# A chunked-softmax attention on one core: keys dealt over the key tiles so that one weight tile serves a whole head

## The chip, the cores and the metric

The kernel runs on one core of a Trainium2 chip. Its time is the device time in microseconds, from the first to the last instruction of that core with what the launch adds, as the median of several runs. Engines: TensorE (PE, with its weight loads as PEld), VectorE (DVE), ScalarE (ACT), GpSimd (POOL), and SyncE (SP), whose queue issues the DMAs that matter here.

## The reference, cut to what matters

Two layers of a small transformer over 2 batches of 1024 tokens, width 128, all in float32. The change is in the attention of the first layer: 16 heads of width 64, of which each group of four shares one key and value head, and the softmax is not over all 1024 keys but inside each chunk of 64 keys.

```
q = (x @ w_q.T) ; k = (x @ w_k.T) ; v = (x @ w_v.T)        # 16 heads of q, 4 of k and v
kc, vc = k, v cut into C = 16 chunks of 64 keys
scores = einsum('bhqd,bhckd->bhcqk', q, kc) * 64 ** -0.5
w = softmax(scores, axis=-1)                               # inside each chunk
chunk_out = einsum('bhcqk,bhckd->bhcqd', w, vc)
sum_w = w.sum(axis=-1, keepdims=True)
out = (chunk_out * sum_w).sum(axis=2) / (sum_w.sum(axis=2) + 1e-09)
```

So each key of a chunk gets the same factor for a given query: a number per (chunk, query), made of the sum of that chunk's exponents and of the total over the chunks. Behind this attention come a soft mixture of experts, a causal attention and a routed mixture, which the change leaves alone.

## The kernel before, in words

One loop runs over the two batches. In it the first attention runs over 16 heads (`head0` on TensorE and VectorE, `head` on ScalarE), each over 8 key tiles of 128 keys. Keys lie on the partitions of the score tiles, the 1024 queries on the free axis. Nothing schedules the work but the order in which each engine's program is written, and semaphores.

What one head costs, and where it is written (lines of the kernel before):

- Maxima: for each of 16 units (a tile of 128 queries by 512 keys) one fp32r matmul (L750, two PSUM banks in turn) and one VectorE reduction to 8 chunk maxima (L1919). Head i works on the units of head i+1, two units after each key tile. Eight transposes (L757) turn them into 16 rows, which ScalarE copies under the queries (L1460).
- Scores of key tile t: two matmuls of the high parts (L771) and two of the low parts with the chunk maxima (L776), then one exponent over 128x1024 on ScalarE (L1502) into EE.
- Chunk sums: at the head's end 16 float32 matmuls of 512 columns with 32 columns of weights (L786), four at a time in the four column groups of the array, since each key tile holds two other chunks. A float32 matmul is two instructions in the profile.
- Normalisers: ScalarE copies the sums out (L1482, 512 columns), four transposes (L796), seven small VectorE operations (L1928 to L1940), four transposes back (L803), a ScalarE copy into `r_rows` (L1477, 512 columns).
- Weights: SP writes `r_rows` into the DRAM tensor `weight_rows` (L503, four DMAs), waits for them (L523/L524), and reads them back spread over partitions: for each key tile two rows, each broadcast to 64 partitions, 256 KB a DMA, 16 DMAs and 4 MB a head (L515), into a ring of four tiles. From the fifth tile on a load waits until VectorE has used the tile it replaces (L512).
- Weighing: VectorE multiplies each EE tile by its weight tile (L1948), tiles 0 to 3 of head i-1 in head i at t = 5 and 7, tiles 4 to 7 in head i+1 at t = 1 and 3. TensorE then sums the values (L814, float32), ScalarE copies them out (L1468).
- Projections of what is needed next stand in the heads at t = 3 and t = 5: queries (L677) in heads 0, 2, 4, ..., keys (L682, two float32 matmuls of 512 columns, moving operand `att_in`) in heads 1, 5, 9, values (L688, eight float32 matmuls, `att_in` as the stationary operand, 64 columns moved) in heads 3, 7, 11. The first group's stand ahead of head 0. The high and low parts of the keys are split on ScalarE (L1448) and VectorE (L1903).

Behind head 15 come its normalisers, the last 12 weighings and values, and the output projection (L881).

Of the kernel before, what the change touches and what calls it, by code (L numbers as in the profile page):

```python
# [12 lines left out]
AX = mybir.AxisListType.X  # L13
ds = bass.ds


P = 128
NB = 2
T = 1024
# [16 lines left out]
CQ = NC // 2  # L36
# [3 lines left out]
              "eps_row": NT, "chunk": 4 * 32}  # L40
# [26 lines left out]
def layer_program(nc, A, out, sorted_in, sorted_out, weight_rows):  # L67
    ctx = ExitStack()
    with ctx:
# [16 lines left out]
        chunk_sum = const("chunk").rearrange("p (a c) -> p a c", a=4)  # L86
# [53 lines left out]
        weight_ring = [v[:, :, :].rearrange("p t d -> p (t d)").rearrange("p (o q) -> p o q", o=2) for v in V1]  # L140
# [15 lines left out]
        S_sb = own0[:, 2 * BANK:3 * BANK]  # L156
        r0 = sb("r0", [P, 4, 4, CQ])
        sw = sb("sw", [P, 4, 4, CQ])
        r1 = sb("r1", [P, 4, 4, CQ])
        tot = sb("tot", [P, 4, 2])  # L160
        rp = sb("rp", [P, 4, 4, 32])
        r_rows = sb("r_rows", [P, BANK])
# [201 lines left out]
        wt_in = [sem(f"wt_in{i}") for i in range(4)]  # L364
# [84 lines left out]
        def _(sp):  # L449
# [33 lines left out]
            with sp.Fori(0, NB) as b:  # L483
                for L in range(2):
                    if L == 0:
# [11 lines left out]
                        def weight_rows_out(i):  # L497

                            sp.wait_ge(s_rr, b * HEADS + i + 1)
                            sp.sem_inc(s_held, 1)  # L500
                            for j in range(4):
                                half, odd = divmod(j, 2)
                                sp.dma_start(weight_rows[i % 2, odd * CQ:(odd + 1) * CQ, half * BANK:(half + 1) * BANK],  # L503
                                             r_rows[32 * j:32 * j + CQ, :]).then_inc(wr_in, 16)
# [16 lines left out]
                        for i in range(HEADS):  # L521
# [3 lines left out]
                            for a in range(4):  # L525
                                if a == 3 and i % GH == GH - 1 and i // GH + 2 < GROUPS:
                                    next_group(i // GH + 2)
                                weight_tiles_in(i, a)
# [102 lines left out]
        def _(pe):  # L631
# [31 lines left out]
            def attention0(b):  # L663
# [3 lines left out]
                krows = HD + NC  # L667
                h0 = b * HEADS
# [68 lines left out]
                def maxima(i, units):  # L737
# [3 lines left out]
                    for x in units:  # L741
# [8 lines left out]
                        pe.matmul(banks(5 + x % 2, BANK), Q_HIGH[u][:, t * P:(t + 1) * P], KA[g % 2][:, half * BANK:(half + 1) * BANK],  # L750
# [29 lines left out]
                def chunk_sums(i, a):  # L780
# [1804 lines left out]
```

## Time and profile before

| | |
|---|---|
| median of 3 runs | 2207.07 us (2201.11 to 2214.0) |
| the profiled execution's own time | 2210.59 us |
| its span, first to last instruction | 2208.5 us |
| granted TensorE clock, mean | 0.932 |
| first attention, batch 0 | about 22 to 532 us, batch 1 about 1110 to 1618 us |

The page's first part says how busy each engine is, part 4 what the chain of work that ended last ran through, and part 5 the costliest groups of instructions with the idle time in front of them. Idle time counts only where the engine is the one that others wait for.

### The profile page before, as it was taken

How to read it: one execution, taken by the hardware profiler on the slowest of the kernel's cores; microseconds unless marked ns; L12 is line 12 of the kernel's file. 1: busy time of each engine (PE TensorE's matmuls, PEld its weight loads, DVE VectorE, ACT ScalarE, POOL GpSimd, SP SyncE). 2: the span in 40 equal slices, each digit the busy share in tenths (PEclk: the TensorE clock that was granted, in tenths of full speed). 3: DMA queues.
4: the chain of work that ended last, by engine and by line, in shares of the span. 5: the costliest groups of instructions: out<-in, count | busy, mean ns of one | idle time of the engine just before them, and what ended most of it. 6: DMA issues, size and time to landing. Idle time of an engine off the chain costs nothing.

```text
span 2208.5 us, 32078 instructions
## 1 busy us (share of the span) xinstructions
PE 1976.8 (90%) x10106; PEld 1193.3 (54%) x10106; DVE 1440.1 (65%) x2492; ACT 980.7 (44%) x1377; POOL 586.5 (27%) x549
## 2 busy tenths in 40 slices
PE   6899999996997999998888999999979889999985
PEld 4444444444784655556644444444448755655554
DVE  7677788865327777753467887778561377777443
ACT  3444454441224666662334444444413246656422
POOL 0000000000101798884120000000010047897921
PEclk7999999998887999998879999999979879999987
DMA  2366665567000000000516565656750000000024
GB/s 94 84 154 160 155 149 141 139 161 237 24 1 10 2 10 6 1 1 30 163 39 154 141 146 141 146 141 151 182 198 1 1 10 10 1 6 1 1 79 135
DMA packets 84846, 187.99 MB, mean 85 GB/s; under 512 B 17697, under 2 KB 46754, under 8 KB 83106
## 3 DMA queue, kind: packets, MB, share of 16 engines
q1 hardware_dynamic: 83650, 183.76, 32.8%
q0 software_dynamic: 1024, 2.10, 0.3%
q8 instruction: 88, 1.44, 0.3%
q14 instruction: 84, 0.69, 0.1%
HBM read 178.47 MB, written 8.91 MB: 85 GB/s over the span
## 4 chain that ended last, share of the span: by engine, by line
PE 67%; DVE 14%; issue 9%; ACT 3%; DMA 3%; POOL 2%; SPq 1%; DVEq 0%; another core or an unknown queue 0%; POOLq 0%; ACTq 0%
PE PS L814 10%; PE PS L786 5%; PE PS L750 5%; PE PS L986 4%; PE PS L926 4%; PE PS L966 3%; DVE mx L1919 3%; PE PS L881 3%; PE PS L969 3%; PE PS L1159 3%; PE PS L771 3%; PE PS L776 3%; PE PS L1218 2%; DMA V<-weight_rows 2%; POOL Esum L2463 2%
## 5 line engine op out<-in xcount | busy, mean ns | idle before, releaser
L1919 DVE TENSOR_REDUCE mx<-PS 128x8 f32<-128x512 f32 x512 | 329.6, 686 | 178.7 <-PE PS L750 164.0
L2463 POOL TENSOR_TENSOR Esum<-Esum,EE 128x512 f32<-128x512 f32 (+3 forms) x320 | 341.3, 1094 | 15.5 <-POOL Esum L2463 10.5
L1948 DVE TENSOR_TENSOR EE<-EE,V 128x1024 f32<-128x1024 f32 x256 | 303.1, 1219 | 45.3 <-DMA V<-weight_rows 44.7
L1502 ACT ACTIVATE EE<-PS 128x1024 f32<-128x1024 f32 x256 | 259.9, 1024 | 142.7 <-PE PS L776 141.2
L2052 DVE TENSOR_REDUCE mrow<-PS 128x1 f32<-128x512 f32 (+3 forms) x384 | 204.1, 552 | 99.1 <-PE PS L929 69.9
L2405 POOL TENSOR_TENSOR QA<-hT,QA 128x512 fp32r<-128x512 f32 x2 | 2.6, 1282 | 996.5 <-ACT hT L1690 996.5
L814 PE MATMUL PS<-EE,Vlater 128*64 128x512 f32 x1024 | 250.5, 609 | 9.4 <-ACT U L1468 8.3
L750 PE MATMUL PS<-KA,QA 128*128 128x512 f32 x512 | 204.1, 454 | 31.8 <-DVE mx L1919 25.8
L1586 ACT ACTIVATE EE<-PS 128x1024 f32<-128x1024 f32 (+2 forms) x192 | 138.1, 739 | 121.4 <-PE PS L969 118.7
L771 PE MATMUL PS<-QA,KA 128*128 128x512 f32 x512 | 185.1, 443 | 0.0
L750 PEld LDWEIGHTS PS<-KA,QA 128*128 128x128 f32 x512 | 97.8, 196 | 130.3 <-DVE mx L1919 88.4
L776 PE MATMUL PS<-QB,KB 80*128 80x512 f32 x512 | 163.1, 400 | 0.0
L986 PE MATMUL PS<-EE,V 128*64 128x512 f32 (+3 forms) x640 | 131.2, 522 | 0.0
L2077 DVE COPY_PREDICATED EE<-consts,F 128x256 f32<-128x256 int32 x96 | 95.3, 992 | 47.9 <-ACT EE L1586 47.8
L814 PEld LDWEIGHTS PS<-EE,Vlater 128*64 128x64 f32 x1024 | 61.8, 136 | 115.3 <-issue 92.4
L786 PE MATMUL PS<-EE,consts 128*32 128x512 f32 x1024 | 116.5, 595 | 0.8 <-DVE QA L1896 0.8
L771 PEld LDWEIGHTS PS<-QA,KA 128*128 128x128 f32 x512 | 91.9, 192 | 42.6 <-issue 26.8
L776 PEld LDWEIGHTS PS<-QB,KB 80*128 80x128 f32 x512 | 98.1, 192 | 22.3
L926 PE MATMUL PS<-KA,QA 128*128 128x512 f32 (+1 forms) x192 | 91.1, 475 | 19.2 <-DVE mrow L2052 12.3
L2454 POOL TENSOR_TENSOR Esum<-F,consts 128x1024 f32<-128x1024 f32 x32 | 62.2, 1965 | 93.5 <-PE PS L1010 62.4
L926 PE MATMUL PS<-KC,QC 128*128 128x512 f32 (+1 forms) x192 | 84.4, 440 | 0.6
L926 PEld LDWEIGHTS PS<-KA,QA 128*128 128x128 f32 x192 | 38.3, 199 | 72.4 <-DVE mrow L2052 50.1
(321 smaller groups left out, 3373.6 us busy)
## 6 DMA issues: line engine op xcount, KB each, us to landing
V<-weight_rows SPq DMA_DIRECT2D x512, 256.0 KB, 5.4
EE<-in_w SPq DMA_DIRECT2D x48, 192.0 KB, 2.7
V<-in_Wg SPq DMA_DIRECT2D x4, 1024.0 KB, 6.4
EE<-in_Wu SPq DMA_DIRECT2D x4, 1024.0 KB, 11.8
EE<-in_Wd SPq DMA_DIRECT2D x4, 1024.0 KB, 13.5
sorted_out<-U SPq DMA_DIRECT2D x12, 256.0 KB, 3.1
wo<-in_wo SPq DMA_DIRECT2D x5, 512.0 KB, 4.4
wq_s<-in_wq SPq DMA_DIRECT2D x17, 128.0 KB, 2.8
```

Source lines behind the costliest of these rows:

```text
L750: pe.matmul(banks(5 + x % 2, BANK), Q_HIGH[u][:, t * P:(t + 1) * P], KA[g % 2][:, half * BANK:(half + 1) * BANK], start=True, stop=True).t ...
L771: pe.matmul(banks(own, hi - lo, lo), KA[g % 2][:, t * P:(t + 1) * P], Q_HIGH[u][:, lo:hi], start=True, stop=False)
L776: mm = pe.matmul(banks(own, hi - lo, lo), KB[g % 2][0:krows, t * P:(t + 1) * P], Q_LOW[u][0:krows, lo:hi], start=False, stop=True)
L786: mm = pe.matmul(PS[32 * j:32 * j + 32, 4 * BANK:5 * BANK], chunk_sum[:, a, :], EE[i % 2][:, 2 * a + odd, half * BANK:(half + 1) * BANK], ...
L814: mm = pe.matmul(PS[HD * half:HD * half + HD, 7 * BANK:8 * BANK], V0[i // GH % 2][:, t, :], EE[i % 2][:, t, half * BANK:(half + 1) * BANK] ...
L926: mm = pe.matmul(banks(4 + h, hi - lo), M1[h][p % 2][:, t * P:(t + 1) * P], S1[h][p % 2][:, lo:hi], start=True, stop=not own)
L986: mm = pe.matmul(PS[HD * h:HD * h + HD, 6 * BANK + lo:6 * BANK + hi], V1[g % 2][:, t, at:at + HD], e_tile(t)[:, h, lo - t * P:hi - t * P], ...
L1502: act.activation(EE[i % 2][:, t, :], banks(2 * (t % 2)), ACT.Exp, scale=QSCALE).then_inc(s["p2_exp"], 1)
L1919: dve.tensor_reduce(mx[:, t, half * 8:half * 8 + 8], banks(5 + x % 2, BANK).rearrange("p (c k) -> p c k", c=8), AX, ALU.max).then_inc(s["p ...
L1948: dve.tensor_tensor(EE[i % 2][:, t, :], EE[i % 2][:, t, :], weight_ring[a % 2][:, odd, :], ALU.mult).then_inc(p3_mul, 1)
L2052: dve.tensor_reduce(mrow1[:, h, t, half:half + 1], banks(4 + h, width), AX, ALU.max).then_inc(s["mx_red"], 1)
L2463: ins = pool.tensor_tensor(Esum[:, h, lo:hi], Esum[:, h, lo:hi], e_tile(t)[:, h, lo - t * P:hi - t * P], ALU.add)
```

## The change

Keys are dealt out instead of cut: key tile t holds the tokens 8k + t for k = 0 to 127, in the order of k. Chunk c is the tokens 64c to 64c + 63, so it has eight keys in every tile, on partitions 8c to 8c + 7. Then the factor of partition p is that of chunk p // 8 in every tile, and one weight tile of 128x1024 serves all eight key tiles of a head.

What follows from it:

- `att_in` is read with a step of 8 elements (32 bytes) by the key projection (as the moving operand) and by the value projection (as the stationary operand). Queries keep their order.
- The maxima read the keys in eight runs of 64 columns, and the reduction takes eight runs of eight per chunk, over two axes.
- Chunk sums: one 128x32 matrix for all tiles, 32 matmuls of 256 columns in place of 16 of 512. The sums are 16 chunks by four quarters of the queries, so the two copies have 256 columns in place of 512, and there are two transposes in place of four, both ways. VectorE's normaliser operations stay at 128 elements.
- Weights: four DMAs to DRAM (16 rows of 256 in place of 8 of 512), then four DMAs of 128 KB, each from 4 rows repeated 8 times to 32 partitions, in place of 16 of 256 KB. The weight tile is double (by the head's parity), and a load waits for the last weighing two heads back. All eight weighings wait for all four DMAs.

```diff
-        weight_ring = [v[:, :, :].rearrange("p t d -> p (t d)").rearrange("p (o q) -> p o q", o=2) for v in V1]
+        weights = [V1[0][:, 4 * i:4 * i + 4, :].rearrange("p t d -> p (t d)") for i in range(2)]
...
-                        def weight_tiles_in(i, a):
-
-                            for odd in range(2):
-                                t = 2 * a + odd
-                                if i >= 1 or t >= 4:
-                                    sp.wait_ge(p3_mul, 1 + (b * HEADS + i) * NT + t - 3)
-                                    sp.sem_inc(s_held, 1)
-                                for k in range(2):
-                                    row = weight_rows[i % 2, odd * CQ + 2 * a + k, :]
-                                    sp.dma_start(weight_ring[a % 2][HD * k:HD * k + HD, odd, :],
-                                                 row.partition_broadcast(HD)).then_inc(wt_in[t % 4], 16)
+                                sp.dma_start(weight_rows[i % 2, :, j * QUARTER:(j + 1) * QUARTER],
+                                             r_rows[32 * j:32 * j + NC, :]).then_inc(wr_in, 16)
+
+                        def weights_in(i):
+
+                            if i >= 2:
+                                sp.wait_ge(p3_mul, 1 + (b * HEADS + i - 1) * NT)
+                                sp.sem_inc(s_held, 1)
+                            for j in range(4):
+                                rows = weight_rows[i % 2, 4 * j:4 * j + 4, :]
+                                sp.dma_start(weights[i % 2][32 * j:32 * j + 32, :],
+                                             rows.unsqueeze(1).to_broadcast([4, CP, T])).then_inc(wt_in, 16)
...
+                by_place = x_in[:, :].rearrange("p (k t) -> p t k", t=NT)
...
-                    pe.matmul(banks(bank, BANK), wk_s[:, 0, :], x_in[:, half * BANK:(half + 1) * BANK],
+                    pe.matmul(banks(bank, BANK), wk_s[:, 0, :], by_place[:, :, half * HD:(half + 1) * HD],
                               start=True, stop=True).then_inc(s["proj_k"], 1)
...
-                        mm = pe.matmul(banks(bank, HD, t * HD), x_in[:, t * P:(t + 1) * P], wv_s[:, 0:HD],
+                        mm = pe.matmul(banks(bank, HD, t * HD), by_place[:, t, :], wv_s[:, 0:HD],
                                        start=True, stop=True)
...
-                        pe.matmul(banks(5 + x % 2, BANK), Q_HIGH[u][:, t * P:(t + 1) * P], KA[g % 2][:, half * BANK:(half + 1) * BANK],
+                        keys = KA[g % 2][:, :].rearrange("p (t k) -> p t k", t=NT)[:, :, half * HD:(half + 1) * HD]
+                        pe.matmul(banks(5 + x % 2, BANK), Q_HIGH[u][:, t * P:(t + 1) * P], keys,
...
-                    pe.wait_ge(s["p2_exp"], 1 + (h0 + i) * NT + 2 * a + 2)
-                    for half in range(2):
-                        for odd in range(2):
-                            j = 2 * half + odd
-                            mm = pe.matmul(PS[32 * j:32 * j + 32, 4 * BANK:5 * BANK], chunk_sum[:, a, :],
-                                           EE[i % 2][:, 2 * a + odd, half * BANK:(half + 1) * BANK],
-                                           start=(a == 0), stop=(a == 3))
+                    pe.wait_ge(s["p2_exp"], 1 + (h0 + i) * NT + t + 1)
+                    for j in range(4):
+                        mm = pe.matmul(PS[32 * j:32 * j + 32, 4 * BANK:4 * BANK + QUARTER], chunk_sum,
+                                       EE[i % 2][:, t, j * QUARTER:(j + 1) * QUARTER], start=(t == 0), stop=(t == NT - 1))
...
-                    for k in range(4):
+                    for k in range(2):
                         mm = pe.transpose(banks(4, P, k * P), S_sb[:, k * P:(k + 1) * P], ident)
...
-                                          banks(5 + x % 2, BANK).rearrange("p (c k) -> p c k", c=8),
-                                          AX, ALU.max).then_inc(s["p1_max"], 1)
+                                          banks(5 + x % 2, BANK).rearrange("p (t c k) -> p c t k", t=NT, k=CP),
+                                          AXY, ALU.max).then_inc(s["p1_max"], 1)
...
-                    dve.wait_ge(wt_in[t % 4], ((h0 + i) * 2 + t // 4 + 1) * 32)
-                    dve.tensor_tensor(EE[i % 2][:, t, :], EE[i % 2][:, t, :], weight_ring[a % 2][:, odd, :],
-                                      ALU.mult).then_inc(p3_mul, 1)
+                    dve.wait_ge(wt_in, (h0 + i + 1) * 64)
+                    dve.tensor_tensor(EE[i % 2][:, t, :], EE[i % 2][:, t, :], weights[i % 2], ALU.mult).then_inc(p3_mul, 1)
```

TensorE's program from the end of head 0 to the projection in head 1, before. Names are destination and source, then output rows by columns; a matmul stands here once, though float32 ones are two instructions in the trace.

```order
388 L814 MATMUL PS<-EE,Vlater 64x512 x4
389 L727 REGISTER_ALU
390 L786 MATMUL PS<-EE,consts 32x512 x12
391 L782 REGISTER_ALU
392 L786 MATMUL PS<-EE,consts 32x512 x4
393 L750 MATMUL PS<-KA,QA 128x512 x2
394 L796 MATMUL PS<-consts,Vlater 128x128 x4
...
409 L814 MATMUL PS<-EE,Vlater 64x512 x4
410 L803 MATMUL PS<-consts,rp 128x128 x4
```

And the same place now.

```order
393 L811 MATMUL PS<-EE,Vlater 64x512 x4
394 L726 REGISTER_ALU
395 L784 MATMUL PS<-EE,consts 32x256 x24
396 L782 REGISTER_ALU
397 L784 MATMUL PS<-EE,consts 32x256 x4
398 L782 REGISTER_ALU
399 L784 MATMUL PS<-EE,consts 32x256 x4
400 L750 MATMUL PS<-KA,QA 128x512 x2
401 L793 MATMUL PS<-consts,Vlater 128x128 x2
...
416 L811 MATMUL PS<-EE,Vlater 64x512 x4
417 L800 MATMUL PS<-consts,rp 128x128 x2
```

Nothing changes place; the sums are twice as many and half as wide, and each row of four transposes is two.

SP's queue for one head, before: the rows out, then the reads into the ring with a wait between them.

```order
47 L503 DMA weight_rows<-r_rows 8x512 x4
48 L523 REGISTER_ALU
49 L511 ISA
50 L515 DMA V<-weight_rows 64x1024 x2
51 L511 REGISTER_ALU
52 L515 DMA V<-weight_rows 64x1024 x4
53 L511 REGISTER_ALU
54 L515 DMA V<-weight_rows 64x1024 x2
...
62 L515 DMA V<-weight_rows 64x1024 x2
```

SP's queue for a head now.

```order
43 L504 DMA weight_rows<-r_rows 16x256 x4
44 L522 REGISTER_ALU
45 L510 ISA
46 L514 DMA V<-weight_rows 32x1x1024 x4
```

The twelve further reads and their waits are gone, and nothing is queued behind a wait for this head's own weighings.

## Rows read from the trace of the kernel before

**Rows 1.** The page's busy time by engine (share of the span, instructions).
```profile
PE 1976.8 (90%) x10106; PEld 1193.3 (54%) x10106; DVE 1440.1 (65%) x2492; ACT 980.7 (44%) x1377; POOL 586.5 (27%) x549
```

**Rows 2.** Stretches: length, busy by engine, PEclk, DMA share, GB/s.
```profile
286.20:287.00 0.80, 0.80 (x5) 0.36 (x3) 0.80 (x2) 0.00 (x0) 0.00 (x0) 1.00 0.72 266
287.00:294.00 7.00, 7.00 (x27) 3.74 (x26) 5.88 (x9) 4.56 (x7) 0.00 (x0) 1.00 1.04 239
282.90:284.50 1.60, 1.60 (x7) 0.83 (x5) 1.49 (x3) 1.23 (x2) 0.00 (x0) 1.00 0.23 41
```

**Rows 3.** Chain of waits, head 8: start, us, what.
```profile
273.65 0.44 PE PS L750
...
277.85 0.69 DVE mx L1919
...
280.96 0.59 PE PS L803 x4
...
286.47 1.06 PE PS L677 x2
...
299.83 3.57 PE PS L786 x32
```

**Rows 4.** Who waited for whom, 75 to 530 us: total, times, longest.
```profile
DVE EE L1948 <- DMA V<-weight_rows: 22.0, 16, 5.5
PEld PS L814 <- DVE EE L1948: 5.2, 8, 1.3
PE PS L814 <- DVE EE L1948: 0.6, 2, 0.4
```

**Rows 5.** TensorE in order of time, heads 7, 15 and after: start, us, idle.
```profile
257.48 2.00 PE L688 MATMUL PS<-wv_s,att_in 128*128 128x64 f32 x16
477.81 0.66 PE L796 MATMUL PS<-consts,Vlater 128*128 128x128 f32 x4 [0.72 <-ACT Vlater L1482]
493.90 1.94 PE L814 MATMUL PS<-EE,Vlater 128*64 128x512 f32 x8 [1.39 <-ACT U L1468]
515.08 1.08 PE L814 MATMUL PS<-EE,Vlater 128*64 128x512 f32 x4
```

**Rows 6.** ScalarE groups, 0 to 540 us, by shape: xcount, busy, mean ns.
```profile
L1502 ACT ACTIVATE EE<-PS 128x1024 f32<-128x1024 f32 x128 | 129.9, 1024 | 71.0 <-PE PS L776 70.3
L1477 ACT ACTIVATE r_rows<-PS 128x512 f32<-128x512 f32 x16 | 9.6, 597 | 49.4 <-PE PS L803 49.4
```

**Rows 7.** TensorE in order of time, values with 128 columns and column groups.
```profile
738.62 1.53 PE L999 MATMUL PS<-F,Vlater 128*64 128x128 f32 x24
739.98 0.39 PE L999 MATMUL PS<-F,V 128*64 128x128 f32 x4
```

**Rows 8.** Groups by shape: the projections, and reductions on VectorE.
```profile
L682 PE MATMUL PS<-att_in,wk_s 128*128 128x512 f32 x32 | 19.7, 701 | 9.0 <-DVE att_in L1883 5.7 <-issue 3.1
L688 PEld LDWEIGHTS PS<-wv_s,att_in 128*128 128x128 f32 x128 | 15.1, 192 | 5.9 <-issue 5.9
L2236 DVE TENSOR_REDUCE U<-U 128x16 f32<-128x128 f32 x2 | 0.7, 367 | 0.1
L2246 DVE TENSOR_REDUCE U<-U 128x16 f32<-128x128 f32 x2 | 0.6, 286 | 0.1
L2052 DVE TENSOR_REDUCE mrow<-PS 128x1 f32<-128x512 f32 x192 | 126.1, 683 | 30.5 <-PE PS L926 26.8 <-PE PS L929 2.9
L2052 DVE TENSOR_REDUCE mrow<-PS 128x1 f32<-128x128 f32 x64 | 17.2, 288 | 11.7 <-PE PS L929 10.6
```

**Rows 9.** In order of time, head 8: rows out, reads in, first weighing.
```profile
281.67 0.60 ACT L1477 ACTIVATE r_rows<-PS 128x512 f32<-128x512 f32 x1 [3.26 <-PE PS L803]
285.06 4.93 SPq L515 DMA_DIRECT2D V<-weight_rows  x8
292.69 2.35 DVE L1948 TENSOR_TENSOR EE<-EE,V 128x1024 f32<-128x1024 f32 x2
```

**Rows 10.** The ring's reads (L515), issue to landing.
```profile
DMA to landing us min/median/max: 3.3/5.4/8.5
```

More of the change, by code:

```diff
@@ L13 @@
 AX = mybir.AxisListType.X
+AXY = mybir.AxisListType.XY
 ds = bass.ds
@@ L35 @@
 EPS_TOTAL = 1e-9
-CQ = NC // 2
+CP = CHUNK // NT
+QUARTER = T // 4
 CONST_COLS = {"ident": 128, "neg": 128, "mask": 128, "first": 16, "after": NT,
-              "eps_row": NT, "chunk": 4 * 32}
+              "eps_row": NT, "chunk": P}
 CONST_AT = {}
@@ L85, in layer_program @@
         neg_fr = sb("neg_fr", [P, P], FR)
-        chunk_sum = const("chunk").rearrange("p (a c) -> p a c", a=4)
+        chunk_sum = const("chunk")[:, 0:32]
         ones_row = sb("ones_row", [1, P])
@@ L154, in layer_program @@
         mx1 = sb("mx1", [P, NT, 33])
[L156 to L162, printed above, removed]
+        S_sb = own0[:, 2 * BANK:2 * BANK + QUARTER]
+        r0 = sb("r0", [P, 2, 4, NC])
+        sw = sb("sw", [P, 2, 4, NC])
+        r1 = sb("r1", [P, 2, 4, NC])
+        tot = sb("tot", [P, 2, 4])
+        rp = sb("rp", [P, 2, 4, 32])
+        r_rows = sb("r_rows", [P, QUARTER])
         with nc.sbuf_tensor("QA2", [P, T], FR) as QA2, nc.sbuf_tensor("QB2", [P, T], FR) as QB2, \
@@ L363, in layer_program @@
         wr_in = sem("wr_in")
-        wt_in = [sem(f"wt_in{i}") for i in range(4)]
+        wt_in = sem("wt_in")
         p3_mul = sem("p3_mul")
@@ L524, in _ @@
                             sp.sem_inc(s_held, 1)
[L525 to L528, printed above, removed]
+                            weights_in(i)
+                            if i % GH == GH - 1 and i // GH + 2 < GROUPS:
+                                next_group(i // GH + 2)
                     else:
@@ L801, in turn_normalisers @@
                     pe.wait_ge(rp_out, h0 + i + 1)
-                    for k in range(4):
+                    for k in range(2):
                         mm = pe.transpose(banks(4, P, k * P), rp[:, k, :, :].rearrange("p j c -> p (j c)"), ident)
@@ L840, in head0 @@
                     bank_four_free(i)
-                    for a in range(4):
-                        chunk_sums(i, a)
+                    for t in range(NT):
+                        chunk_sums(i, t)
                     if i + 2 < HEADS:
@@ L1447, in high_k @@
                     act.wait_ge(s["proj_k"], 1 + 2 * (g0 + g) + half + 1)
-                    act.activation(KA[g % 2][:, half * BANK:(half + 1) * BANK], banks(bank, BANK),
+                    keys = KA[g % 2][:, :].rearrange("p (t k) -> p t k", t=NT)[:, :, half * HD:(half + 1) * HD]
+                    act.activation(keys, banks(bank, BANK).rearrange("p (t k) -> p t k", t=NT),
                                    ACT.Copy).then_inc(s["k_hi"], 1)
@@ L1476, in normalisers @@
                         act.wait_ge(wr_in, (h0 + i) * 64)
-                    act.activation(r_rows[:, :], banks(4, BANK), ACT.Copy).then_inc(s_rr, 1)
+                    act.activation(r_rows[:, :], banks(4, QUARTER), ACT.Copy).then_inc(s_rr, 1)
                 def sums(i):
                     act.wait_ge(s_full, 1 + h0 + i + 1)
-                    act.activation(S_sb[:, :], banks(4, BANK), ACT.Copy).then_inc(s_copy, 1)
+                    act.activation(S_sb[:, :], banks(4, QUARTER), ACT.Copy).then_inc(s_copy, 1)
                 def high_next(i, half, h):
@@ L1797, in row_under_k, with first_chunk_under_k @@
                                   ALU.mult, ALU.add)
+            def first_chunk_under_k(h, lo, hi, value):
+                row = KB[h][HD:HD + 1, :].rearrange("p (t k) -> p t k", t=NT)[:, :, lo:hi]
+                dve.tensor_scalar(row, consts[HD:HD + 1, lo:hi].unsqueeze(1).to_broadcast([1, NT, hi - lo]), 0.0, value, ALU.mult, ALU.add)
             def modulation():
@@ L1901, in low_k @@
                     dve.wait_ge(s["k_hi"], 1 + 2 * (g0 + g) + half + 1)
-                    cols = slice(half * BANK, (half + 1) * BANK)
-                    dve.tensor_tensor(KB[g % 2][0:HD, cols], banks(bank, BANK, rows=HD), KA[g % 2][0:HD, cols],
+                    low, high = [k[g % 2][0:HD, :].rearrange("p (t k) -> p t k", t=NT)[:, :, half * HD:(half + 1) * HD]
+                                 for k in (KB, KA)]
+                    dve.tensor_tensor(low, banks(bank, BANK, rows=HD).rearrange("p (t k) -> p t k", t=NT), high,
                                       ALU.subtract).then_inc(s["k_lo"], 1)
@@ L2337, in _ @@
                 for h in range(2):
[L2338 to L2340 removed]
+                    first_chunk_under_k(h, 0, CP, 1.0)
+                    first_chunk_under_k(h, CP, P, 0.0)
                 attention0(b)
@@ L2504, in const_array @@
     put("eps_row", rows)
-    a = np.arange(4)[None, :, None]
-    col = np.arange(32)[None, None, :]
-    put("chunk", (col == 2 * a + (np.arange(P) // CHUNK)[:, None, None]).reshape(P, 4 * 32))
+    put("chunk", q == p // CP)
     k = np.arange(T)[None, :]
-    own_chunk = ((p - HD) == k // CHUNK).astype(np.float32)
+    own_chunk = ((p - HD) == k % P // CP).astype(np.float32)
     return c, own_chunk
```

23 lines of the change are left out of this document (8 added, 15 removed).

## The prediction

> **What bounds the kernel now.** I read four views, in this order. The page's busy times put TensorE far ahead of every other engine [rows 1]. The chain of waits through one head in the middle (head 8, 273.6 to 303.4 us) shows what a head's 29.75 us consist of: TensorE nearly throughout, with two stretches on other engines. At the head's start the chain leaves TensorE after the two first maxima, goes through VectorE (reductions, the normaliser's small steps, one more reduction that starts at 277.85) and comes back; it doesn't pass the transposes of the sums. Further on it holds the four transposes of the normalisers, the two projections and the 32 instructions of the chunk sums [rows 3]. The waits say what the ring of weight tiles costs: VectorE stood 22.0 us for its DMAs in batch 0, but TensorE, which sets the end, stood only 5.2 and 0.6 us for the weighed tiles [rows 4]. So 117 MB of DMA traffic that disappear are worth little by themselves; the share of 1.04 and 239 GB/s of a stretch with the ring running [rows 2] are no bound of anything. The last view is order of time in the tail: after 515.08 TensorE goes from values to output projection without a gap [rows 5], so earlier weights would not pull in the end.
>
> **The change part by part.** The sum is made against the profiled execution's 2210.59 us (span 2208.5 and 2.1 around it), which is 3.5 above the median of 2207.07.
>
> *Transposes and copies, -8.4.* On the chain stand four transposes back in 0.59 us, with the latency of one in it; four issue in about 0.42, so two fewer take 0.21 off [rows 3]. That is in 15 of 16 heads: 14 x 0.21 = 2.9 for heads 1 to 14. The two fewer transposes of the sums and the shorter copy gain nothing in heads 0 to 14, since VectorE's reduction at 277.85 is what is late next there and nothing of its steps gets shorter (the normaliser keeps its 128 elements). They do count where no maxima are left to cover them, ahead of head 15 and behind it: the copy goes from 512 to 256 columns, at (1024 - 597)/512 = 0.83 ns a column 0.21 less [rows 6], of the 0.72 us that TensorE stands for it [rows 5], and 0.21 for the transposes. Twice 0.42, and once more 0.21 and 0.25 at the last normalisers: 1.3. Together 4.2 a batch, 8.4 in all.
>
> *Chunk sums, +3.2.* 64 instructions of 256 columns for 32 of 512: the same columns, 3.57 us on the chain [rows 3]. What can differ is the rate of short ones. The trace has no four column groups at 256 columns. Bounds: nothing more, or the nearest row, 128 columns in two groups, which go at (739.98 - 738.62)/24 = 56.7 ns each with a weight load each [rows 7]; 64 x 56.7 = 3.63, against 3.57 with the latency of one in it, which is up to 0.2 more. I take 0.1 a head, 32 heads.
>
> *Reading att_in with a step of 32 bytes, +25.* No TensorE instruction of the trace reads with a step. The nearest rows are two reductions of VectorE over the same 128 elements to 16 results: L2246 reads them in line, 286 ns, L2236 with a step of 64 bytes, 367 ns [rows 8]. That is 0.63 ns an element on top of VectorE's (683 - 288)/384 = 1.03 ns [rows 8], 1.66 ns an element. TensorE takes 3.57/8/512 = 0.87 ns a float32 column in line [rows 3], so if memory gives a stepped element every 1.66 ns, each column costs 0.79 more. Key projection: 32 instructions x 512 columns x 0.79 = 12.9 us. Value projection: 16 instructions in 2.00 us [rows 5], about 0.115 each, which is the load of 128 columns and not the 64 that are moved; 128 loads x 128 x 0.79 = 12.9 us. In the heads nothing covers them: ScalarE's next exponent and VectorE's next reduction both follow TensorE there. Ahead of head 0 about 0.4 us a batch stay beside other waits. So 25. Bounds: 0 if TensorE reads stepped rows at its rate, 27 if it takes twice the time. The row of the same memory with a step says that a step costs, so I take it.
>
> The row shows that a step of 64 bytes makes an element 1.6 times as long on VectorE. The Trainium skill (Advanced Engine Details and Errata, SBUF Cachelines) has lines of 16 bytes and full rate only with at least two hits on one; 32 bytes is a new line for every element, so by that rule the key and value projections pay as above. Without it and without the row's cost, the sum would be 25 lower.
>
> *Other stepped operands, 0.* The maxima's keys go in runs of 64, the reduction in runs of 8 at one element a time as now. If the reduction over two axes were slower, each 0.1 us would cost about 0.9 us a head, since some nine of a head's 16 are near the chain; bounds 0 and 0.63 ns an element, 0.3 us each.
>
> *Arrival of the weights, +12.* The 128 descriptors of 4 KB are a tenth of before, but VectorE now waits for all, at the first weighing. Before: r_rows is done at 282.27, the first read is issued at 285.06 (2.8 later), the first weighing is at 292.69 [rows 9]; so 10.4 us are there, 9.5 in heads 5 and 9 and 8.6 to 9.1 in heads 13 and 14. A read of 256 KB lands in 3.3 at best [rows 10]. At 266 GB/s and a share of 0.72 an engine does 4 KB in 0.177 us, at 239 GB/s and 1.04 in 0.285 [rows 2]; four of these in the 3.3 leave 2.6 fixed. How many of the 16 DMA engines the new reads get no row shows: their source is 4 rows, each 8 times. The nearest row is the writing of 8 rows at a time, which kept 0.23 x 16 = 3.7 engines busy [rows 2]. I take four engines, which is 32 packets one behind the other. Then the weights are there 2.8 + 2.6 + 32 x 0.177 = 11.1 us after r_rows. Against the time there is (0.25 more than before, for r_rows is earlier, and 0.8 to 1.7 more in heads with a stepped projection) heads 1, 5, 9 lose up to 0.8 each, heads 13 and 14 about 2, and the last two sets of weights 2 each, where TensorE waits for values at once: up to 9.7 a batch. Each 0.1 us of landing is worth 0.5 of it, and with few engines drawing I expect somewhat under 0.177, so 6 a batch. Bounds: with 16 engines the weights are there before they are wanted, 0; at 0.285 a packet 14.5 us after r_rows, 3 to 4 us in every head, over 100 in all.
>
> By the Trainium skill (DMA: Bandwidth & Descriptors, Why a DMA increments its semaphore by 16 and not by 1) a DMA runs on the largest number up to 16 that divides the slowest dimension of both sides. Here that is 4 of the source and 32 of the destination, so 4, and 16 for each read of the old ring. By the rule the term is as taken; without it the sum would be 12 lower.
>
> Sum: 2210.6 - 8.4 + 3.2 + 25 + 12 = 2242.4; less 3.5, the median should be about 2239.
>
> **The rivals.**
>
> *Stepped reads are free on TensorE* (the other side: no slower by what can be measured). Then -8.4 + 3.2 + 12, or -5 where the weights also arrive in time: 2214 and 2202. For it: TensorE's float32 instructions move an element only every 0.87 ns, so memory may keep up; and no TensorE row speaks against it. Against it: the VectorE row. It decides from the point at which a stepped element costs less than 0.25 ns more (25 x 0.25/0.79 = 8 us).
>
> *The weights come late in every head.* If four engines reach only the 0.285 us a packet of the full ring, VectorE stands 3 us at t = 5 in each head, the maxima behind it and TensorE's transposes of them follow: some 45 more a batch, about 2330. Against it: 0.285 belongs to 16 engines drawing together 239 GB/s, and four draw under 100.
>
> *Losing the traffic helps.* VectorE's 22.0 us a batch for the ring [rows 4] go, of which TensorE felt 5.8, and the reads are free of each other. With free stepped reads and 16 engines: 2202 less up to 8, 2194. Against it: what TensorE felt lies at places where the new weights are no earlier (heads 1 and 15, tail).
>
> *The reduction over two axes costs.* At 0.1 us more, 0.9 x 30 = 27 on top of the sum, 2266. Against it: it reads eight elements in a row.
>
> **How the numbers follow.** The forecast (steps cost about as on VectorE, four engines, little lateness) 0.50, with its own range 2222 to 2256; free steps 0.26 (most of it 2214, some 2202); late in every head 0.09; traffic helps 0.06; slow reduction 0.09. What a measurement of this kernel can tell from no change is 0.5%, or 11 us: faster is under 2196, slower over 2218. Faster: 0.06 and a little of the free steps, 0.08. Same: most of the free steps and the low edge of the forecast, 0.26. Slower: 0.66. The range that leaves two in ten out runs from 2202, the free case with all in time, to 2265, which takes in the upper bound of the steps, half of the lateness bound of 9.7 and a slightly slower reduction.
>
> **What would show it.** Key projection: instructions of L681 about twice 0.43 us apart, and the two with the latency at 1.5 to 1.9 instead of 1.1. Value projection: 16 instructions in 3.5 instead of 2.00. If both stand as before, the 25 is wrong. Heads with a query projection should keep 29.7 us or lose 0.2; key heads should go from 28.9 to about 30.5. The sums should stay at 3.5 to 3.8 us. VectorE should wait for the weights in heads 13 and 14 and in the tail, once a head; a DMA share of a quarter while they load says four engines, a short burst of a full share says 16. Reductions should keep 686 ns. The forecast is wrong if the maxima's matmuls, reading eight runs, take longer, or if the sums are bound by their weight loads.

## The result, and the profile after

| | before | after |
|---|---|---|
| median | 2206.9 us (4 runs) | 2250.9 us (4 runs, 2230.2 to 2252.6) |
| ratio to before, 95% interval | | 1.0183 [1.0155, 1.0211] |
| span of the profiled execution | 2208.5 us | 2250.8 us |
| granted TensorE clock, mean | 0.932 | 0.922 |

Slower, by about 40 us. The forecast was 2239 in a range of 2202 to 2265. The page first, busy time by engine, against [rows 1]:

```profile
PE 2002.9 (89%) x11002; PEld 1228.9 (55%) x11002; DVE 1433.9 (64%) x2488; ACT 968.1 (43%) x1377; POOL 586.5 (26%) x549
```

TensorE is 26 us busier, VectorE 6 less; so part of the loss is work and part is waiting. Groups by line in the whole execution (busy, mean ns of one):

```profile
L1922 DVE TENSOR_REDUCE mx<-PS 128x8 f32<-128x512 f32 x512 | 329.3, 685 | 215.6 <-PE PS L750 204.4
L784 PE MATMUL PS<-EE,consts 128*32 128x256 f32 x2048 | 118.4, 383 | 0.8 <-DVE QA L1898 0.8
L681 PE MATMUL PS<-att_in,wk_s 128*128 128x512 f32 x32 | 33.2, 1126 | 9.3 <-DVE att_in L1885 5.7 <-issue 3.4
L687 PEld LDWEIGHTS PS<-wv_s,att_in 128*128 128x128 f32 x128 | 31.2, 333 | 7.5 <-issue 7.5
```

The reduction over two axes takes 685 ns, as before. The two stepped projections are what grew: a key instruction from 701 to 1126 ns, a weight load of the value projection from 192 to 333 [rows 8].

TensorE in order of time shows what a head costs (start, duration, count). The first four rows are the chunk sums that end heads 3 to 6, the rest is head 7 with its value projection:

```profile
160.97 3.66 PE L784 MATMUL PS<-EE,consts 128*32 128x256 f32 x64
190.50 3.66 PE L784 MATMUL PS<-EE,consts 128*32 128x256 f32 x64
221.10 3.66 PE L784 MATMUL PS<-EE,consts 128*32 128x256 f32 x64
250.63 3.66 PE L784 MATMUL PS<-EE,consts 128*32 128x256 f32 x64
...
266.82 4.02 PE L687 MATMUL PS<-wv_s,att_in 128*128 128x64 f32 x16
270.65 1.14 PE L771 MATMUL PS<-QA,KA 128*128 128x512 f32 x2
271.58 1.06 PE L776 MATMUL PS<-QB,KB 80*128 80x512 f32 x2
272.44 1.06 PE L750 MATMUL PS<-KA,QA 128*128 128x512 f32 x2
273.29 1.02 PE L771 MATMUL PS<-QA,KA 128*128 128x512 f32 x2
274.14 0.64 PE L776 MATMUL PS<-QB,KB 80*128 80x512 f32 x2
...
282.70 3.66 PE L784 MATMUL PS<-EE,consts 128*32 128x256 f32 x64
```

A query head takes 29.53 us (190.50 to 160.97), a key head 30.60, the value head 32.07. In the kernel before the same sums stand here:

```profile
152.79 3.64 PE L786 MATMUL PS<-EE,consts 128*32 128x512 f32 x32
182.51 3.64 PE L786 MATMUL PS<-EE,consts 128*32 128x512 f32 x32
211.36 3.64 PE L786 MATMUL PS<-EE,consts 128*32 128x512 f32 x32
241.10 3.64 PE L786 MATMUL PS<-EE,consts 128*32 128x512 f32 x32
270.01 3.64 PE L786 MATMUL PS<-EE,consts 128*32 128x512 f32 x32
```

That is 29.72, 28.85 and 28.91. So the query head gained 0.2, the key head lost 1.75, and the value head 3.2, of which 2.0 are the projection's own ([rows 5] has it at 2.00, here 4.02). The rest is in the rows behind it: the same instructions take 1.06 instead of 0.63 us. The windows name the reason (columns as [rows 2]; PEclk is the third from the end):

```profile
267.00:270.70 3.70, 3.70 (x17) 3.70 (x17) 1.11 (x1) 0.00 (x0) 0.00 (x0) 1.00 0.26 91
270.70:274.10 3.40, 3.40 (x9) 2.71 (x9) 0.99 (x2) 1.62 (x2) 0.00 (x0) 0.50 0.14 55
```

The granted clock falls from 2.4 to 1.2 GHz for 3.4 us, right behind 3.8 us of weight loads that each moved only 64 columns. Five of the six value heads of this execution have such a stretch behind the projection (head 3 of batch 0 has none), of 3.4 us in batch 0 and 6.8 in batch 1. In the kernel before no value head has one. It has one at all, in head 1 of batch 0, where TensorE had waited 3.11 us and the values behind take 3.58 instead of 1.94:

```profile
89.66 1.04 PE L757 MATMUL PS<-consts,mx 128*16 128x128 f32 x8 [3.11 <-DVE mx L1919]
90.63 3.58 PE L814 MATMUL PS<-EE,Vlater 128*64 128x512 f32 x8
```

The last part is waiting. Who waited for whom, 75 to 560 us, and TensorE at heads 14 and 15 and in the tail of batch 0:

```profile
DVE EE L1950 <- DMA V<-weight_rows: 21.4, 8, 8.0
```

```profile
491.63 1.04 PE L757 MATMUL PS<-consts,mx 128*16 128x128 f32 x8 [1.20 <-DVE mx L1922]
...
515.63 3.02 PE L811 MATMUL PS<-EE,Vlater 128*64 128x512 f32 x8 [2.74 <-DVE EE L1950]
518.58 4.29 PE L784 MATMUL PS<-EE,consts 128*32 128x256 f32 x64
...
539.59 1.08 PE L811 MATMUL PS<-EE,Vlater 128*64 128x512 f32 x4 [1.03 <-DVE EE L1950]
```

And VectorE and SP there:

```profile
506.81 2.60 SPq L514 DMA_DIRECT2D V<-weight_rows  x4
...
514.26 2.36 DVE L1950 TENSOR_TENSOR EE<-EE,V 128x1024 f32<-128x1024 f32 x2 [8.04 <-DMA V<-weight_rows]
```

The window of the clock at that wait:

```profile
515.60:519.00 3.40, 3.37 (x12) 0.72 (x16) 3.29 (x3) 0.00 (x0) 0.00 (x0) 0.63 0.02 5
```

VectorE waits about as long as before (21.4 against 22.0 us [rows 4]). What is new is how TensorE meets it: it stands 2.74 us in one piece at 515.63, and the values behind take 3.02 instead of 1.94 us, since the clock falls here too. Behind the shorter wait of 1.20 us at 491.63 the same values take 1.94. While such a set of weights loads, DMA works at this share:

```profile
508.00:514.00 6.00, 4.89 (x21) 2.34 (x19) 0.00 (x0) 3.93 (x5) 0.00 (x0) 1.00 0.24 87
```

0.24 x 16 engines is 3.8, so about four.

**Where the 42.3 us between the two spans are.** From the start to the sums of head 0, +5.0, of which 1.3 is there before the first changed instruction starts (22.56 before, 23.86 after). From there to the end of the sums of head 15, +44.4 in both batches together: +19 for the steps at full clock (six value heads x 2.0, four key heads x 1.75), +11 for half clock in the value heads and in head 2 of batch 1, +17 in heads 1, 13, 14 and 15, where the weights are late, and -2 in the query heads. The other stretches sum to -7, although the two tails in them lose 2; what is gained there is not the change's. Between the attentions of the two batches, where the kernels are the same, TensorE is at half clock for 143 us before and 133 us after, and from 120 to 157 us in the profiled executions of the experiments; a single run moves by 10 us with that.

### The profile page after: what moved, and what is told of

Its sections match the earlier page's. It is cut to its first block, busy times and chain, and to the rows that moved or that the text cites. A ratio compares the mean times of both kernels' runs of the same rounds, so it can differ in the third digit from the quotient of the medians.

```text
span 2250.8 us, 33040 instructions
## 1 busy us (share of the span) xinstructions
PE 2002.9 (89%) x11002; PEld 1228.9 (55%) x11002; DVE 1433.9 (64%) x2488; ACT 968.1 (43%) x1377; POOL 586.5 (26%) x549
## 3 DMA queue, kind: packets, MB, share of 16 engines
q0 software_dynamic: 1024, 2.10, 0.3%
## 4 chain that ended last, share of the span: by engine, by line
PE 65%; DVE 14%; issue 9%; DMA 4%; ACT 3%; POOL 2%; SPq 2%; another core or an unknown queue 1%; DVEq 0%; POOLq 0%; ACTq 0%
PE PS L811 9%; PE PS L784 5%; PE PS L750 4%; PE PS L983 4%; PE PS L923 4%; DVE mx L1922 4%; PE PS L963 3%; PE PS L966 3%; PE PS L1156 3%; PE PS L878 2%; PE PS L771 2%; DMA V<-weight_rows 2%; PE PS L776 2%; PE PS L1215 2%; POOL Esum L2463 2%
## 5 line engine op out<-in xcount | busy, mean ns | idle before, releaser
L1950 DVE TENSOR_TENSOR EE<-EE,V 128x1024 f32<-128x1024 f32 x256 | 300.2, 1218 | 42.8 <-DMA V<-weight_rows 42.3
L1500 ACT ACTIVATE EE<-PS 128x1024 f32<-128x1024 f32 x256 | 260.1, 1024 | 152.3 <-PE PS L776 150.5
L811 PE MATMUL PS<-EE,Vlater 128*64 128x512 f32 x1024 | 260.5, 631 | 13.0 <-DVE EE L1950 8.0
L771 PE MATMUL PS<-QA,KA 128*128 128x512 f32 x512 | 195.3, 463 | 0.0
L750 PEld LDWEIGHTS PS<-KA,QA 128*128 128x128 f32 x512 | 100.5, 201 | 129.9 <-DVE mx L1922 97.0
L784 PE MATMUL PS<-EE,consts 128*32 128x256 f32 x2048 | 118.4, 383 | 0.8 <-DVE QA L1898 0.8
L784 PEld LDWEIGHTS PS<-EE,consts 128*32 128x32 f32 x2048 | 63.3, 111 | 68.6 <-issue 29.0
```

Source lines behind the costliest of these rows:

```text
L771: pe.matmul(banks(own, hi - lo, lo), KA[g % 2][:, t * P:(t + 1) * P], Q_HIGH[u][:, lo:hi], start=True, stop=False)
L784: mm = pe.matmul(PS[32 * j:32 * j + 32, 4 * BANK:4 * BANK + QUARTER], chunk_sum, EE[i % 2][:, t, j * QUARTER:(j + 1) * QUARTER], start=(t ...
L811: mm = pe.matmul(PS[HD * half:HD * half + HD, 7 * BANK:8 * BANK], V0[i // GH % 2][:, t, :], EE[i % 2][:, t, half * BANK:(half + 1) * BANK] ...
L1500: act.activation(EE[i % 2][:, t, :], banks(2 * (t % 2)), ACT.Exp, scale=QSCALE).then_inc(s["p2_exp"], 1)
L1950: dve.tensor_tensor(EE[i % 2][:, t, :], EE[i % 2][:, t, :], weights[i % 2], ALU.mult).then_inc(p3_mul, 1)
```

## The experiments

In what follows a ratio is to the kernel before, measured beside each set of kernels (medians 2204.5 and 2205.4), and "us back" is the difference between such a ratio and the 1.0183 of after. One per cent is 22 us. Of the two kernels on the size of the step there is one run each, with one of the kernel before at 2202.6. The values computed differ in four kernels that read other tokens in the projections: `in_line`, `neither`, `values_in_line`, `before_stepped`, and in the two on the size of the step.

**Steps undone** (e1_in_line; e8_neither is the same kernel, run once more).

```
- pe.matmul(banks(bank, BANK), wk_s[:, 0, :], by_place[:, :, half*HD:(half+1)*HD], ...)
+ pe.matmul(banks(bank, BANK), wk_s[:, 0, :], x_in[:, half*BANK:(half+1)*BANK], ...)
- mm = pe.matmul(banks(bank, HD, t*HD), by_place[:, t, :], wv_s[:, 0:HD], ...)
+ mm = pe.matmul(banks(bank, HD, t*HD), x_in[:, t*P:(t+1)*P], wv_s[:, 0:HD], ...)
```

> The changed kernel with the key and the value projection reading att_in in line, as before; keys are then not dealt over the tiles, so the values computed differ, while every other instruction stands as in the changed kernel. Theory (stepped reads, and the clock that falls behind them): in the profile after, a stepped key instruction takes about 0.98 us for 0.43 and a stepped weight load 0.238 for 0.114, 32 x 0.55 + 128 x 0.124 = 33.5 us, and value heads show a stretch at half clock, about 1.8 us each in six of them; all goes, 2251 - 33.5 - 11 = 2206. Rival (what costs is the late arrival of the weights, the steps stand beside other waits): 2235 or more.

Measured 2228.1 us, ratio 1.0122 [1.0098, 1.0147]: 13 us back of the 40, not 45. TensorE's wait for VectorE ahead of the transposes of the maxima shows why (75 to 560 us; after, it was 11.5 us in all and 2.7 at the longest):

```profile
DVE EE L1950 <- DMA V<-weight_rows: 28.8, 11, 8.2
PE PS L757 <- DVE mx L1922: 18.7, 14, 4.9
```

With the steps gone the key and value heads should fall to 28.7 us, and they stay at 28.8 to 29.5, heads 12 to 15 of batch 0 at 30.2, 33.5, 29.1 and 24.8. Wherever VectorE waits for the weights they come 10.6 to 12.5 us after `r_rows`, and the steps had been covering that. The second run of it:

> The changed kernel with projections in line (the values computed differ) once more, a look: where the steps are gone, theory says that the weights are what is late in every key head and query head (first weighing 10.5 to 11 us after r_rows whatever the head), so key heads take 29.3 and not 28.7 us. Rival: 28.7.

2236.7 us in one run, the key heads again at 29.1 to 29.6. Head 3, a value head, takes 34.8 and 34.9 us in the two batches: its weights come 14 us after `r_rows`, TensorE stands 3.98 us, and half clock follows though nothing is read with a step.

```profile
156.76 1.88 PE L757 MATMUL PS<-consts,mx 128*16 128x128 f32 x8 [3.98 <-DVE mx L1922]
```

Why they come so late in this head is not shown. The steps and the lateness lie side by side, so neither undone alone gives back its own size.

**Value steps undone** (e2_values_in_line: the second half of the edit above).

> The changed kernel with only the value projection reading in line (its values computed differ); keys are still read with the step. Theory: -128 x 0.124 = -16 and the half clock of the value heads goes, -11: about 2224, value heads at 28.9 us or less, key heads still at 30.6. Rival (the half clock in value heads has nothing to do with the stepped loads): 2235, with a stretch of half clock still in those heads.

2226.8 us, 1.0127 [1.0095, 1.016], 12 us back by the ratio. Value heads at 28.8 to 29.3, key heads at 30.6 as in after, and no half clock in a value head.

**Value steps kept, split** (e4_values_in_halves: tiles 0 to 3 at t = 3, 4 to 7 at t = 5).

```
- project_v(g, 4)                                     # at t = 3, all eight tiles
+ project_v(g, 4, range(4 * half, 4 * half + 4))      # at t = 3 and at t = 5
```

> The changed kernel with the stepped value projection in two parts, tiles 0 to 3 at t = 3 and 4 to 7 at t = 5, as the key projection is; same instructions, same reads. Theory (3.8 us of nothing but loads with 64 columns each let the granted clock fall): two parts of 1.9 us don't, the value heads lose 1 to 2 us each: about 2240. Rival (only the load rate costs; the clock falls anyway or for another reason): 2251, half clock still in those heads.

2238.1 us, 1.0143 [1.0122, 1.0165]. Each half takes its stepped time, and the clock stays up:

```profile
265.71 2.12 PE L687 MATMUL PS<-wv_s,att_in 128*128 128x64 f32 x8
267.63 0.71 PE L772 MATMUL PS<-QA,KA 128*128 128x512 f32 x2
```

```profile
267.00:275.00 8.00, 8.00 (x34) 5.50 (x34) 4.94 (x7) 2.17 (x3) 0.00 (x0) 1.00 0.15 55
```

After the same work in one piece the instruction at 270.65 took 1.14. Five of the six value heads take 30.8 us instead of 30.9 to 33.2 (one 31.4), and none has half clock. The profiled execution as a whole is the slowest of seven (2255.7 us), with 150 us at half clock between the attentions, so what is read from it are the heads and not the time.

So half the work at a time doesn't pull the clock down. All of it at once may, but need not: it did in 5 of 6 value heads after, in 5 of 6 with the steps alone, in 2 of 6 with one DMA, and in 3 of 6 in each of the two kernels on the size of the step, 18 of 30. The next experiment's head 3 is one where it didn't, with the same 4.02 us and full clock behind:

```profile
141.44 4.02 PE L685 MATMUL PS<-wv_s,att_in 128*128 128x64 f32 x16
145.27 0.71 PE L769 MATMUL PS<-QA,KA 128*128 128x512 f32 x2
```

What decides between the two is not shown.

**The weights by one DMA** (e3_sixteen_engines).

```
- for j in range(4):
-     rows = weight_rows[i % 2, 4*j:4*j + 4, :]
-     sp.dma_start(weights[i % 2][32*j:32*j + 32, :], rows.unsqueeze(1).to_broadcast([4, CP, T])).then_inc(wt_in, 16)
+ sp.dma_start(weights[i % 2], weight_rows[i % 2, :, :].unsqueeze(1).to_broadcast([NC, CP, T])).then_inc(wt_in, 16)
- dve.wait_ge(wt_in, (h0 + i + 1) * 64)
+ dve.wait_ge(wt_in, (h0 + i + 1) * 16)
```

> The changed kernel with the weight tile read by one DMA whose source is 16 rows, each 8 times, to 128 partitions, instead of four with 4 rows each. Theory (each of the four small DMAs ran on four engines, 32 packets of 0.159 us one behind the other): now 8 packets an engine on all 16; weights are there about 7 us after r_rows instead of 10.6, VectorE waits for them nowhere but in the last head; the tail and heads 13 and 14 give back 2.7 + 1.0 + about 3 a batch and the half clock there, 2251 - 16 = 2235. Rival (the number of engines is not set by the source's rows, or the waits are beside others): landing as before, 2250.

2219.1 us, 1.0066 [1.0043, 1.0089]: 26 us back, more than expected. The wait, and the share while the set loads (0.47 and 0.45 are means that take in the start and the end; half-microsecond windows from 518.5 to 520.5 have 0.86 to 1.26, so all engines draw):

```profile
DVE EE L1948 <- DMA V<-weight_rows: 8.8, 2, 4.9
```

```profile
517.20:519.50 2.30, 2.24 (x13) 1.01 (x12) 0.43 (x1) 0.68 (x2) 0.00 (x0) 1.00 0.47 144
519.50:521.50 2.00, 2.00 (x21) 2.00 (x20) 0.05 (x1) 1.45 (x2) 0.00 (x0) 1.00 0.45 104
519.50:520.00 0.50, 0.50 (x7) 0.50 (x6) 0.00 (x0) 0.50 (x2) 0.00 (x0) 1.00 0.86 221
```

The 512 KB land in 4.2 us where four engines took over 7. Heads 13 to 15 of batch 0 go from 31.3, 28.7, 24.1 to 28.1, 27.8, 21.7, and head 1 from 29.3 to 25.2: a head that the prediction had priced at 0.8 at most, because in the kernel before the ring made it 27.9. Half clock is left in one value head a batch, and that is 7 us of the 34 between the two profiled executions, beside 8 in head 1, 13 in heads 13 to 15 and 5 in the tails.

**Two rows a DMA** (e7_two_rows: eight DMAs with a source of two rows).

```
- for j in range(4): rows = weight_rows[i % 2, 4*j:4*j + 4, :]
+ for j in range(8): rows = weight_rows[i % 2, 2*j:2*j + 2, :]
...                                            # to 16 partitions each; VectorE waits for all eight
```

> The changed kernel with the weight tile read by eight DMAs of 2 rows, each 8 times, to 16 partitions. Theory (the rows of the source set how many DMA engines work): two engines, 64 packets of 0.159 us one behind the other, 5 us more than with four; weights are there 15.5 us after r_rows, nearly 5 us later in all heads but the value heads, so 2251 + 2 x (12 x 4.5 + 2 x 2) = 2365, and a DMA share of 0.13 while they load. Rival (eight small DMAs run on other engines each, or always on four): landing at 10.6 to 11 us, 2250 to 2258.

2447.6 us, 1.1109 [1.1063, 1.1156]. The weights are there 15.6 us after `r_rows` and more, as worked out for two engines, but a head takes 34 to 38 us, more than the wait explains. TensorE at the end of a head:

```profile
283.90 1.88 PE L757 MATMUL PS<-consts,mx 128*16 128x128 f32 x8 [5.63 <-DVE mx L1922]
285.70 2.56 PE L811 MATMUL PS<-EE,Vlater 128*64 128x512 f32 x8
```

```profile
283.00:293.00 10.00, 9.10 (x86) 4.48 (x87) 5.26 (x8) 1.40 (x2) 0.00 (x0) 0.80 0.01 2
```

Behind the wait of 5.63 us the clock is down (eight transposes in 1.88 us instead of 1.04), and so in nearly every head. The two attentions with their tails hold 253 us at half clock, where after has 58; half of the difference, some 97 us of lost work at most (an estimate), is about the 82 that were missing. A long wait of TensorE costs more than its length.

**Before, with the steps alone** (e5_before_stepped: the two `by_place` reads in the kernel before).

> The kernel before, whose key and value projections alone read att_in with the step of the changed kernel (the values computed differ); ring, sums and transposes as before. Theory (the steps cost by themselves 32 x 0.55 + 128 x 0.124 = 33.5 us, and where 3.8 us of stepped value loads stand in one piece some half clock behind them): 2204.5 + 33.5 + 3 to 12 = 2241 to 2250. Rival (steps only hurt together with the late weights): under 2225.

2234.8 us, 1.0125 [1.0088, 1.0163]: +28 by the ratio (19 to 36), under the size I had written and over the rival's. Key heads at 30.8, value heads at 31.0 in one case and 32.2 in five, those with half clock behind the projection. This is the price of the steps with the ring's weights as they were. Head 1 takes 26.3 and 26.0, no longer than before.

**Both mended** (e6_dealt_once: one DMA; GpSimd copies `att_in` once a batch into the new order, and groups 1 to 3 read the copy in line).

```
+ pool.tensor_copy(x_placed.rearrange("p (t k) -> p t k", t=NT),
+                  att_in[:, :].rearrange("p (k t) -> p t k", t=NT)).then_inc(x_dealt, 1)
...                                            # the keys alike, and one DMA as above
- by_place[:, t, :], wv_s[:, 0:HD],
+ (placed if g else stepped)[:, t, :], wv_s[:, 0:HD],
```

> The changed kernel with the weight tile read by one DMA of 16 rows, and with att_in dealt once a batch by GpSimd into a half of V1 that attention leaves free; key and value projections of groups 1 to 3 read that copy in line, only group 0 still reads with the step. It computes what the reference does. Theory (steps and late weights are all that the change lost, and transposes and copies gain): of the 2219.1 with sixteen engines go three quarters of 33.5 and the half clock of the value heads, 25 + 3: 2191, faster than before. Rival (something else of the change costs too, such as the sums or the reduction over two axes): 2205 or more.

2191.5 us (10 runs), 0.994 [0.9921, 0.996]: 13 us under the kernel before. The copy is 2.09 us on an engine that has nothing else to do there, and the value projection stands as it did:

```profile
22.64 2.09 POOL L2404 COPY V<-att_in 128x1024 f32<-128x1024 f32 x1 [6.00 <-ACT att_in L1423]
...
255.15 2.00 PE L690 MATMUL PS<-wv_s,V 128*128 128x64 f32 x16
```

Heads take 29.5 and 28.7 us, head 1 24.3, and in neither attention does the clock fall.

**Other steps** (e9_short_steps: keys 8 bytes, values 16; e10_long_steps: keys 64).

```
- by_place[:, :, half*HD:(half+1)*HD]
+ x_in[:, half*BANK:(half+1)*BANK].rearrange("p (k t) -> p t k", t=2)     # e10: t=16
- by_place[:, t, :]
+ x_in[:, :].rearrange("p (k t) -> p t k", t=4)[:, t % 4, 0:P]             # e9 alone
```

> After, with the key projection reading with a step of 8 bytes and the value projection with one of 16 bytes (both read other tokens than they should, so the values computed differ). What is disputed is what a step costs TensorE. At 32 bytes a pair of key instructions stands in 2.08 us against 1.12 in line, and 16 value instructions in 4.02 us against 2.00; both are 1.9 ns an element. Theory 1: memory hands over a line at a time and an element that is alone on its line costs 1.9 ns; with a step of 8 bytes a line holds several, so the key pairs should stand in 1.12 to 1.3 us. The value instructions at 16 bytes say how long a line is: 4.02 us if it is 16 bytes, near 2.0 if it is 32 or more. The Trainium skill (Advanced Engine Details and Errata, SBUF Cachelines) has lines of 16 bytes, by which it is 4.0. Theory 2: any step breaks a burst, so the size doesn't matter: 2.08 and 4.02. Time, one look: theory 1 with 16-byte lines about 2240, theory 1 with longer lines 2230, theory 2 2251.

> After, with the key projection reading with a step of 64 bytes instead of 32 (other tokens than it should, so the values computed differ); the value projection as in after. If each element that is alone on its line costs the same, a pair of key instructions stays at 2.08 us and its head at 30.6, time 2251 as after. If the cost grows with the step, a pair takes up to 4 us, each key head 4 us more, 2275. Against the latter speaks that VectorE's 64-byte step cost it less (0.63 ns an element over in line) than TensorE's 32-byte step costs TensorE (1.05).

The first two rows are of the kernel with short steps, the last of the one with long:

```profile
205.24 1.17 PE L681 MATMUL PS<-att_in,wk_s 128*128 128x512 f32 x2
...
264.04 4.00 PE L687 MATMUL PS<-wv_s,att_in 128*128 128x64 f32 x16
```

```profile
206.63 1.97 PE L681 MATMUL PS<-att_in,wk_s 128*128 128x512 f32 x2
```

At 8 bytes 1.17 us (in line 1.12), at 32 bytes 2.08, at 64 bytes 1.97; 16 bytes cost the value projection all that 32 do. By the Trainium skill's lines of 16 bytes (Advanced Engine Details and Errata, SBUF Cachelines) this was to be so, and the durations agree; "any step" falls, and so does a cost that grows with the step. The times were missed for the first: 2256.6 us in one run, not 2240 (2258.3 for the second, 2251 expected). Its clock was 0.919, its key heads 29.2 to 30.4, with late weights as in the experiment with the steps undone. I hold the durations for settled; the times, with one run each, are not.

## Why the prediction was right or wrong

- *Transposes and copies, -8.4.* Right: a query head lost 0.20 us (0.21 forecast). In the kernel with both costs mended, against the kernel before, heads 2 to 15 give 5.5 and the tails 1.8 in both batches, 7.3 of the 8.4; the rest of its 13 us is head 1, next point.
- *The ring's 22 us are worth little by themselves.* Right for the heads in the middle, wrong for head 1, which takes 27.9 and 26.4 us in the two batches before and 24.3 and 24.5 when the weights are in time. That is part of the rival "losing the traffic helps": it holds, some 5 us in both batches, but after never saw it, as its weights were late in head 1 too.
- *Chunk sums, +3.2.* 64 instructions in 3.66 us against 32 in 3.64: +0.02 a head, 0.6 in all. The rate of short instructions is the same, and the sums are not bound by their weight loads.
- *Stepped reads, +25.* The mechanism is right, the price of an element was low, and more of it was covered than I had. A pair of key instructions takes 2.08 us instead of 1.12, and they stand 0.98 apart where 0.43 was; the 16 value instructions take 3.83 us to the next instruction (266.82 to 270.65) instead of 1.81. That is 0.98/512 = 1.91 and 3.83/16/128 = 1.87 ns an element, where VectorE's row had given 1.66. So 32 x 0.55 + 8 x 2.02 = 34 us of TensorE, over the bound of 27 ("if it takes twice the time"): it is 2.2 times. Of these 19 show in the value and key heads and 3 to 4 ahead of batch 0; ahead of batch 1 the engine is at half clock, where a step of the key projection costs next to nothing (last section) and the value projection's 1.9 us more stand beside other waits, and head 1 waits for its weights anyway. So 22 to 23 show where 25 were forecast, by two errors that cancel, which is luck.
- *Where the load is read.* That the value projection pays by its 128 loaded columns and not by the 64 moved was right.
- *Arrival of the weights, +12.* Four engines, right: share 0.24. 11.1 us after `r_rows` was forecast, 10.6 measured (503.66 to 514.26). The places were right too: heads 13 and 14 and the tail. The worth was low: against the kernel before about 19 us are lost in heads 1 and 13 to 15 and the tails, and one DMA instead of four gives 26 back in the runs. The term that was mis-sized is this one. By the prediction's own slope, 0.5 a batch for each 0.1 us of landing, 10.6 us make 7.2 a batch or 14. The slope put head 1 at 0.8 at most, where 4.1 and 3.8 us are lost against the kernel with one DMA, and it left out that TensorE, having waited, works on at half clock. (Its 128 descriptors are an eighth of the 1024 before, not a tenth; the sum doesn't use that.)
- *Late in every head, 2330.* Ruled out for after, whose steps made its heads longer. With the steps undone it shows in key and value heads, by 0.1 to 0.8 us each, and not in query heads, which keep their 29.5.
- *Reduction slower, 2266.* Ruled out, 685 ns against 686. The maxima's matmuls, which read eight runs, keep their median of 398 ns.
- *Not in the sum: the clock.* Half clock behind the value projection costs 1.2 us in two heads of batch 0 and 2.3 in three of batch 1. Head 2 of batch 1 has 3.4 us of it too and loses 1.6, behind a wait of 1.07 us only. Together that is 11 us in the profiled execution. The prediction treated TensorE's rate as given.

The forecast with the sizes measured: 2239 - 2 (steps) - 3 (sums) + 7 (weights) + 11 (clock) = 2252, for a median of 2251. The sizes are read in one execution, and executions differ by 10 us, so the match is no closer than that. The steps' mechanism carried the verdict; what made the forecast 12 too low is the clock, which the sum did not have, and the worth of the late weights, less what the sums did not cost.

## What to carry to other kernels

Before a layout turns a float32 operand into one with a step of 16 bytes or more, price it at 1.9 ns an element at full clock, and copy it once into order if it is read again and an idle engine is there: 2 us of GpSimd a batch took 2219 us to 2191. When a DMA broadcasts few rows to many partitions, let its source have 16 rows; then read off the share in a window whether all engines draw. And where TensorE sets the end, a wait or a stretch of weight loads can cost more than its length: look at the granted clock behind it, and mend costs that lie side by side together, since each undone alone hides the other.

## What the runs showed of the hardware

- The pace of a stepped read doesn't hang on TensorE's clock. Ahead of batch 1 the key projection runs at half clock, the stepped pair and two in-line ones (L676) one behind the other:

```profile
1123.12 2.18 PE L681 MATMUL PS<-att_in,wk_s 128*128 128x512 f32 x2 [3.41 <-issue]
1125.12 1.89 PE L676 MATMUL PS<-att_in,wq_s 128*128 128x512 f32 x2
```

```profile
1121.00:1127.00 6.00, 3.88 (x5) 1.66 (x6) 1.42 (x4) 0.00 (x0) 2.16 (x3) 0.50 0.22 59
```

The in-line pair goes from 1.12 us at 2.4 GHz to 1.89 at 1.2 GHz, the stepped one from 2.08 to 2.18. Before, the same key pair in line at half clock took 2.07 us (1105.57), so there the step is nearly free. What sets the stepped pace doesn't follow TensorE's clock; that it is the memory is the likely reading, and no run shows it by itself.
- A step of 8 bytes costs 0.05 us a pair of 512-column instructions, and 64 bytes cost no more than 32 (1.97 and 2.08 us). For weight loads 16 bytes cost what 32 do (4.00 and 4.02 us for 16).
- With a source of 2 rows, 512 KB take 12.7 us from issue to use, at a share of 0.13; with 4 rows 7.5, at 0.24; with 16 rows 4.2.
- TensorE's granted clock fell to 1.2 GHz behind 3.8 us of stepped loads with 64 columns moved each in 18 of 30 value heads of five kernels, and during or behind waits of 2.7, 3.1, 4.0 and 5.6 us. It stayed at 2.4 GHz behind 1.9 us of the same loads and behind a wait of 1.20 us. In head 2 of batch 1 it fell behind a wait of 1.07 us, so the length of the wait alone doesn't say it.
